# Self-attention scores as pairs of 64-row matmuls of 128 columns into two banks

## What is computed

```python
def _L0_attn_ref(x, Wq, bq, Wk, bk, Wv, bv, Wo, bo):
    EMBED_DIM = 512; NUM_HEADS = 16; HEAD_DIM = 32; NUM_KV_GROUPS = 2; WINDOW = 64
    ...
    q = (xp @ Wq + bq).reshape(B, Lp, H, D).transpose(0, 2, 1, 3)
    k = (xp @ Wk + bk).reshape(B, Lp, G, D).transpose(0, 2, 1, 3)
    ...
    scores = jnp.einsum('brgnqd,bgnkd->brgnqk', qg, kw) * scale
    attn = jax.nn.softmax(scores, axis=-1)
    og = jnp.einsum('brgnqk,bgnkd->brgnqd', attn, vw)
    ...
    return o @ Wo + bo
```

## Time and profile before

| | |
|---|---|
| median of 3 runs | 2766.39 us (2765.36 to 2767.1) |
| profiled execution, its span | 2765.4 us (equal to the fastest of the runs, 2765.36) |
| self-attention | about 0 to 447 us |
| cross-attention, then mixture of experts | the rest |
| score matmuls (L740, `w_ps_s`) | 768, of 128 × 112 stationary and 256 streamed columns |
| mean granted TensorE clock | 0.953 |

### The profile page before, as it was taken

The page is one execution under the profiler, slowest core; times in us unless marked ns, Lnnn a source line. Parts: engine busy times, 40 slices in busy tenths (PEclk is TensorE's granted clock), DMA queues, the critical chain, the costliest instruction groups (busy, mean ns, idle before and its releaser), DMA issues. The chain is left out here.

```text
span 2765.4 us, 56399 instructions
## 1 busy us (share of the span) xinstructions
PE 2589.5 (94%) x16770; PEld 2364.0 (85%) x16771; DVE 1755.7 (63%) x4862; ACT 1294.8 (47%) x3135; POOL 1032.2 (37%) x1426
## 2 busy tenths in 40 slices
PE   6899996899999999999996999999999999988688
PEld 5888886899999999999986899999999999978576
DVE  7888886656666665666664666665666665555466
ACT  4555554545545454554543545454554554441211
POOL 4334433333344433333341444333334344332422
PEclk9999998999999999999998999999999999995599
DMA  3223224111111111111113111111111111103654
GB/s 101 89 72 100 89 94 141 53 37 45 32 32 38 42 32 36 44 34 32 32 30 115 30 33 44 36 32 36 45 32 32 37 43 32 34 16 110 228 173 126
DMA packets 122050, 168.80 MB, mean 61 GB/s; under 512 B 20753, under 2 KB 69329, under 8 KB 121857
## 3 DMA queue, kind: packets, MB, share of 16 engines
q1 hardware_dynamic: 116944, 151.43, 18.3%
q0 software_dynamic: 5040, 16.58, 1.5%
HBM read 111.73 MB, written 56.23 MB: 61 GB/s over the span
## 5 line engine op out<-in xcount | busy, mean ns | idle before, releaser
L1135 POOL TENSOR_SCALAR x_probs<-x_probs,x_inv 112x376 f32<-112x376 f32 x512 | 652.5, 1285 | 237.2 <-DVE x_inv L1308 237.2
L1127 POOL TENSOR_SCALAR x_bias<-x_top 112x1 f32<-112x1 f32 x512 | 117.9, 230 | 977.5 <-DVE x_top L1279 976.5
L1392 PE MATMUL x_ps_f<-x_wo,x_oT 128*112 128x512 f32 x1536 | 374.8, 400 | 1.9 <-DVE x_oT L1294 1.9
L1392 PE MATMUL x_ps_f<-x_xT,x_wq 128*128 128x224 f32 x3072 | 365.8, 275 | 7.0 <-DVE x_xT L1261 7.0
L1392 PEld LDWEIGHTS x_ps_f<-x_xT,x_wq 128*128 128x128 f32 x3072 | 361.8, 193 | 10.4 <-issue 7.4
L1199 ACT ACTIVATE x_probs<-x_probs,x_bias 112x376 f32<-112x376 f32 x512 | 308.1, 604 | 64.1 <-POOL x_bias L1127 57.8
L1392 PEld LDWEIGHTS x_ps_f<-x_wo,x_oT 128*112 128x112 f32 x1536 | 265.3, 176 | 85.0 <-issue 2.2
L1452 PE MATMUL x_ps_o<-x_pT,x_v 128*128 128x224 f32 (+1 forms) x2304 | 315.6, 282 | 2.7 <-DVE x_oT L1294 2.7
L1424 PE MATMUL x_ps_s<-x_kT,x_qT 128*112 128x376 f32 x1536 | 311.4, 338 | 5.4 <-DVE x_wo L1244 5.4
L1392 PE MATMUL x_ps_f<-x_ctxT,x_wk 128*128 128x376 f32 x1536 | 312.7, 340 | 2.5 <-DVE x_ctxT L1250 2.5
L1392 PE MATMUL x_ps_f<-x_wv,x_ctxT 128*128 128x512 f32 (+1 forms) x1152 | 304.9, 400 | 0.0
(11 more groups left out here) (194 smaller groups left out, 3876.0 us busy)
## 6 DMA issues: line engine op xcount, KB each, us to landing
x_ctxn<-in_ctx_dram SPq DMA_DIRECT2D x64, 256.0 KB
x_xf<-h2T SPq DMA_DIRECT2D x32, 448.0 KB, 4.2
m_rows<-slots SPq DMA_DIRECT2D x35, 258.0 KB, 2.9
slots<-w_blank SPq DMA_DIRECT2D x8, 1032.0 KB, 5.2
m_hn<-in_L_ffn_W_dram SPq DMA_DIRECT2D x32, 256.0 KB, 4.9
x_ctxn<-in_ctx_dram SPq DMA_DIRECT2D x64, 119.0 KB
w_xa<-in_x_dram SPq DMA_DIRECT2D x32, 224.0 KB, 3.0
w_xr<-in_x_dram SPq DMA_DIRECT2D x32, 224.0 KB, 3.2
```

Of the source, the lines that this page charges most:

```text
L1127: pool.tensor_scalar(bias[:, m:m + 1], top[:, m:m + 1], -0.1 * NEG, -SCALE, ALU.max, ALU.mult) \
L1135: pool.tensor_scalar(probs[0:T, m, 0:SE], probs[0:T, m, 0:SE], inv[:, m:m + 1], None, ALU.mult).then_inc(normed, 1)
L1392: last = pe.matmul(o, w, x, start=m == 0, stop=m == len(jobs) - 1)
```

## The change

Per batch, the 24 matmuls of 128 rows and 256 streamed columns are replaced by 48 of 64 rows and 128 streamed columns. For each chunk m, window and pass, two matmuls follow each other: one on rows 0 to 63 (the first two heads of the chunk) with columns 0 to 127 of `kd`, into bank 0, and one on rows 64 to 127 (the last two heads) with columns 128 to 255, into bank 1. The omitted quarters of `kd` are zeros, so the scores are the same. Bank u now holds head pairs u of all four chunks, where before it held all heads of two chunks, and fill A reads `pT` in the new order. Both banks are complete only with the last pair, and `scores_ready` is raised twice there. TensorE waits once, before the first pair, for `less_ready` of both banks of the batch before.

```diff
@@ -785,7 +785,7 @@
                         for w, (lo, hi) in enumerate(((0, R0), (R0, T))):
                             last = product(rows[:, :, lo:hi],
                                            [(vd[:, a, s, w, q, :],
-                                             pT[:, b_].rearrange("p (c q) t -> p q c t", q=2)[:, q, :, lo:hi])
+                                             pT[:, b_].rearrange("p (q c) t -> p q c t", q=2)[:, q, :, lo:hi])
                                             for q in range(2) for a, b_ in PASSES])
@@ -803,15 +803,20 @@
                     if s == 0:

                         pe.wait_ge(fill_done, fills.until(turn.before(), ("Q", KC - 1)))
-                    for u in range(2):
-                        if not (turn.reg is None and turn.at == 0 and s == 0):
-
-                            pe.wait_ge(less_ready, turn.count(8, 2 * s + u - 1))
-                        for m in range(2 * u, 2 * u + 2):
-                            last = product(ps_s[u][0:T, (m % 2) * 4 * WIN:(m % 2 + 1) * 4 * WIN],
-                                           [(q[:, a, m, s, :], kd[:, b_, s, w, :])
-                                            for w, q in enumerate((qa, qb)) for a, b_ in PASSES])
-                        last.then_inc(scores_ready, 1)
+                    if not (turn.reg is None and turn.at == 0 and s == 0):
+
+                        pe.wait_ge(less_ready, turn.count(8, 2 * s))
+                    pairs = [(w, a, b_) for w in range(2) for a, b_ in PASSES]
+                    for m in range(KC):
+                        for n, (w, a, b_) in enumerate(pairs):
+                            for u in range(2):
+                                rows = slice(2 * D * u, 2 * D * (u + 1))
+                                last = pe.matmul(ps_s[u][0:T, m * 2 * WIN:(m + 1) * 2 * WIN],
+                                                 (qa, qb)[w][rows, a, m, s, :],
+                                                 kd[rows, b_, s, w, 2 * WIN * u:2 * WIN * (u + 1)],
+                                                 start=n == 0, stop=n == len(pairs) - 1)
+                                if m == KC - 1 and n == len(pairs) - 1:
+                                    last.then_inc(scores_ready, 1)
```

## The result

The changed kernel takes 2781.6 us (median of 4 runs, 2780.4 to 2788.4) against 2766.7 us for the kernel before, a ratio of 1.0057 with a 95% interval of 1.0043 to 1.0071: 15 us slower. The forecast had the direction, but named 2810 us and a mechanism that did not occur. The profiled execution has a span of 2778.7 us, 13.3 us more than before.

A forecast was written before the change was run, and what follows sets the result against it. TensorE was taken to bound steps 0 and 3, VectorE steps 1 and 2. Terms of 1.94, 0.2, 1.5 and 1.94 us gave 5.6 us per turn, 44 over eight: 2810 us, range 2756 to 2840 (own range 2797 to 2825).

The forecast's parts named there:

- What bounds the kernel: Self-attention: TensorE and VectorE both nearly full, busy 367 and 338 of 406 us, so the price depends on the step.
- steps 0 and 3: First and last of a turn's four score groups: TensorE sets the time, so all 1.94 us count in each.
- steps 1 and 2: Middle two of a turn's four score groups: VectorE sets the time; added cost 0.2 and 1.5 us.
- The gap in step 1: TensorE's 1.99 us wait for VectorE's residual addition, taken to hide all 1.94 us of the longer group on TensorE.
- The price of a pair: Score group: a pair's two loads run one after the other, 48 × 0.097 = 4.66 us, 1.74 us more than before.
- the sum: Self-attention: added time of a turn's four score groups, 5.6 us per turn over eight turns, taken as 44 us.
- rival 3: Score groups: doubled loads drop the granted clock below 0.8, adding 38 us to the forecast: 2848 us; chance 0.10.
- rival 1: Score groups: the halves run side by side, a pair costs one load, group 2.53 us: 2760 us; chance 0.28.
- Going in and out of 64-row work: Around each score group: both changes of row mode together cost 0 to 0.4 us per batch, taken as 0.2.
- Rival 2: Score groups: pairs side by side but held by something else, 0.125 to 0.160 us each: 2771 to 2788 us; chance 0.17.
- Rival 4: Score groups: a load of half the rows costs half, 48 × 0.062 side by side, 1.5 us a group: 2747; chance 0.05.
- The late first bank: Both score banks complete only at group end; VectorE loses its early start, called hidden where TensorE is late itself.

The follow-up runs named there:

- serial kernels: Changed kernel's 48 matmuls reordered, all for one bank and then all for the other: 64 rows each, ratio 1.0340; 128 rows each, ratio 1.0143.
- The one with full rows: Changed kernel with 48 matmuls of 128 columns, bank after bank, each over all 128 rows instead of 64: ratio 1.0143 to the kernel before.
- filled kernels: Idle matmuls in TensorE's three gaps per turn and two at the stage's ends: changed kernel 0.9965, kernel before 0.9961, as ratios to the kernel before.
- shorter, thinner group with full rows: Changed kernel with 24 matmuls of 128 rows and 128 columns per batch, half the score products left out: ratio 1.0034 to the kernel before.

## Why the prediction was wrong

**What bounds the kernel** was right: scores in steps 0 and 3 are on TensorE's path, steps 1 and 2 are VectorE's, and VectorE hardly waited for scores. The gap in step 1 was taken for slack that hides added work. It does, but the clock behind it depends on it too, and that was read only for step 3: the one turn that was read is one of two in the loop in which the group of step 2 ran at the upper clock from end to end.

**The price of a pair** is the step that failed first. The prediction took 48 × 0.097 = 4.66 us because its nearest row had loads one after the other; measured were 24 × 0.098. The term was +1.74 us and is −0.57 (24 × 0.098 = 2.35 against 2.92). The row chosen was for loads that use the same rows, and could not speak for loads on different ones. That the price of a single load was right (0.098 us on average, for 0.097) the serial kernels show. The one with full rows bears out most of the rest of the sum: it has the forecast's loads without the 64-row form, and costs 40 us, where the sum without its 0.2 us for that form gives some 38. Step by step it takes 1.9, 0, 0.9 and 1.9 us more than the turn shown before, for 1.7, 0.1, 1.3 and 1.7 in such a sum; its first bank comes early, so the path of step 2 is not tested in full. The forecast's loads with the 64-row form cost 96 us, more than twice the sum, at a mean clock of 0.82.

**The clock** is the other step that failed. The sum had no term for it: it priced every group at the upper level, and kept the clock for rival 3. With the term of the loads put right the sum gives a gain, as rival 1 says, and what was measured is 15 us lost. The runs put this loss at the group of step 2, 4.67 us in place of 2.50, and the O product behind it: with the gap in front of it filled, the ratio falls from 1.0057 to 0.9976.

The page "TensorEngine Tiling (Array Packing)" of the Trainium skill, section "Key Properties", said that tiles can load and multiply in parallel; the trace of after agrees (0.098 us for two loads and two matmuls). The other rule weighed, from the Trainium skill's page "TensorE: Matmul & The Clock Gate", section "LDWEIGHTS (loading the stationary operand)", is that a load costs by its columns and not by its rows; the traces agree (0.098 us on average with 64 rows and with 128). They do not contradict each other, and weighing one against the other was the mistake.

**Going in and out of 64-row work** was 0.2 us in the sum. The runs show 0.16 ahead of the group and 0.10 in it, 0.26 together, inside the bounds of 0 to 0.4. That the 0.10 is the price of leaving the form is a reading of two group lengths and not tried by itself.

**Rival 1** had the mechanism and the group's length (2.53 us forecast, 2.51 measured) and still the wrong time, 2760, as it kept the clock. Even with the clock held it asked too much: it gave 0.39 us each to steps 0 and 3, and the filled kernels show 0.15 and 0.38, less 0.13 in step 1. **Rival 3** had the cause of the time, with its place and its mark (granted clock of the group's window below 0.8; measured 0.50 in step 2), but was added to the forecast's serial loads and priced at 2848. Neither stood alone in the list: the pair side by side *with* the clock lost was given no chance, though each half had one. Rival 2 had nearly the time (2771 to 2788) by a mechanism that did not occur: behind the first of a group no pair takes more than 0.102 us at the upper clock. Rival 4's 0.062 us for a load stands without a working; half of 0.097 would be 0.049. Neither occurred.

**The late first bank** was called hidden in steps 0 and 3, and in steps 1 and 2 the sum had it only as the later end of a longer group (0.2 and 1.5 us). The kernel that makes only this change loses 6 to 7 us (7.0 us of stage), some 2.5 of which remain when the clock is held; step 1 then takes 11.31 us for 11.12, which is the 0.2 us that the sum gave it. The rest fits a longer wait of TensorE in steps 1 and 2 with more half clock behind it (48 us against 41), which is argued from the records and not tried by itself.

Where the 17.6 us of stage went, then, as far as one profiled execution of each kernel tells: +7.0 for both banks late, +3.7 for the shorter, thinner group with full rows (419.6 − 415.9; the group's own gain of 0.5 us and the clock's loss together), +6.9 for the rest (426.5 − 419.6), of which some 3 us are cold stretches that fall in other turns. The first is also shown by the ratio (1.0026). The second is not clear of noise in the total: 1.0034 against 1.0026, with intervals that overlap. The third is 1.0057 against 1.0034, with intervals that just overlap.

## What to carry to other kernels

Two matmuls on different row halves and different banks, issued one behind the other, cost one: but a pair still takes the 0.098 us of one load, so streaming 128 columns in place of 256 saved 0.41 of a group's 2.92 us and not a half. Before making TensorE's work denser or thinner in front of or behind one of its gaps, look up the granted clock of that stretch, in more than one turn: a shorter product next to a gap can be paid for at half speed, here 4.67 us for 2.51. A gap that cannot be closed can be filled with matmuls that nobody reads, which made either kernel of this case 0.4% faster.

## What the runs showed of the hardware that I had not expected

- TensorE without a pause can still fall to 1.2 GHz: with 24 + 24 matmuls of 64 rows, matmul row busy 46.00 of 46 us, the mean clock was 0.81; with 128 rows and the rest of the kernel equal, busy 49.42 of 49.50 us, it was 1.00. The means over the whole kernel part as clearly in every execution: 0.930 to 0.935 against 0.951 to 0.955. In these two kernels the rows that a matmul uses matter beside how long TensorE is busy.
- The two starts of a pair lie 0.003 to 0.004 us apart, loads and matmuls alike, with float32r operands.
- A cold stretch moves. The gap of 1.9 us before the third Q fill is the same in all kernels without idle matmuls in it, and 24 Q matmuls behind it take 5.36 us in some turns and 3.85 or 3.86 in others of one execution: slow 5 times of 7 before, 7 of 7 with both banks late, 4 of 7 in the changed kernel, 3 of 7 with only the gap of step 1 filled.
